# C rows of a Mamba scan: broadcast by DMA from DRAM in pairs, two states per GpSimd multiply

## What is computed

```python
def step(s, inp):
    d_t, u_t, B_t, C_t = inp
    dA = jnp.exp(d_t[..., None] * A)
    s = s * dA + (d_t * u_t)[..., None] * B_t[:, :, None, :]
    y_t = jnp.einsum('bhdn,bhn->bhd', s, C_t)
    return (s, y_t)
```

## Time and profile before

| | us |
|---|---|
| median of 3 runs | 6185.75 (6184.68 to 6187.2) |
| profiled execution, span | 6181.4 |
| VectorE busy | 6057.9 (98%) |
| GpSimd busy | 4848.8 (78%) |
| TensorE matmul busy | 4735.1 (77%) |
| ScalarE busy | 4198.7 (68%) |

### The profile page before, as it was taken

How to read it: one execution, slowest core, us unless ns; L and a number is a source line. 1 busy time by engine, 2 the same in 40 slices (tenths; PEclk the granted TensorE clock), 3 DMA queues, 4 the chain that set the end, 5 groups by cost and what they waited for, 6 DMA issues and landing times.

```text
span 6181.4 us, 90775 instructions
## 1 busy us (share of the span) xinstructions
PE 4735.1 (77%) x14623; PEld 2333.3 (38%) x14892; DVE 6057.9 (98%) x8285; ACT 4198.7 (68%) x7312; POOL 4848.8 (78%) x4113
## 2 busy tenths in 40 slices
PE   4777777777777777777777777777777777777778
PEld 1233333333333333333333333333333333333334
DVE  7999999999999999999999999999999999999998
ACT  5766766676666667666676676666766766676663
POOL 6888777777787778777777787777777877787875
PEclk9999999999999999999999999999999999999999
DMA  1000000000000000000000000000000000000000
GB/s 43 5 8 9 9 9 11 9 9 9 12 8 9 9 12 9 9 9 11 9 9 9 12 9 9 9 11 9 9 9 11 9 9 9 12 9 9 9 6 13
DMA packets 59893, 62.59 MB, mean 10 GB/s; under 512 B 7014, under 2 KB 58342, under 8 KB 59110
## 3 DMA queue, kind: packets, MB, share of 16 engines
q1 hardware_dynamic: 57536, 53.68, 2.8%
q10 hardware_dynamic: 1702, 2.16, 0.1%
HBM read 39.04 MB, written 16.78 MB: 9 GB/s over the span
## 4 chain that ended last, share of the span: by engine, by line
DVE 45%; issue 26%; PE 21%; DVEq 4%; ACT 3%; POOL 1%; another core or an unknown queue 0%; DMA 0%; ACTq 0%; POOLq 0%
DVE state L824 14%; DVE db L814 8%; DVE acc L763 8%; PE ybank L892 6%; PE pbank L901 3%; DVEq L97 3%; PE db L879 3%; PE bank_b L947 2%; DVE v L647 2%; DVE spw L708 2%; PE bank_a L1017 2%; ACT decay L408 1%; DVE hh L758 1%; PE cbank L870 1%; PE bank_a L980 1%
## 5 line engine op out<-in xcount | busy, mean ns | idle before, releaser
L558 POOL TENSOR_TENSOR prod<-state,cs 128x512 f32<-128x512 f32 x2048 | 2777.2, 1356 | 1068.2 <-DVE state L824 1025.6
L395 ACT ACTIVATE cs<-cbank 128x512 f32<-128x512 f32 x2048 | 1217.0, 594 | 1184.3 <-PE cbank L870 993.4
L408 ACT ACTIVATE decay<-delta,aneg 128x512 f32<-128x512 f32 x2048 | 1455.1, 716 | 607.2 <-DVE state L824 599.4
L879 PE MATMUL db<-pieces,sel 128*128 128x512 bf16 x2031 | 807.5, 398 | 1345.7 <-DVE state L824 1309.8
L892 PE MATMUL ybank<-prod,ident 128*128 128x512 f32 x3072 | 1626.7, 619 | 2.7 <-POOL prod L562 2.6
L814 DVE TENSOR_TENSOR db<-db,du 128x512 f32<-128x512 f32 x2048 | 1394.4, 681 | 46.8 <-PE db L879 28.3
L824 DVE TENSOR_TENSOR_SCAN state<-decay,carry,db 128x512 f32<-128x512 f32 x1024 | 1286.7, 1257 | 0.0
L824 DVE TENSOR_TENSOR_SCAN state<-decay,db 128x512 f32<-128x512 f32 x1024 | 1229.3, 1200 | 0.0
L879 PEld LDWEIGHTS db<-pieces,sel 128*128 128x128 bf16 x2048 | 199.5, 97 | 2245.9 <-DVE state L824 2157.8
L562 POOL TENSOR_TENSOR prod<-prod 128x512 f32<-128x512 f32 x512 | 690.7, 1349 | 40.1
L870 PE MATMUL cbank<-pieces,sel 128*128 128x512 bf16 x1797 | 699.2, 389 | 14.9 <-ACT cs L395 13.9
(11 more groups left out here) (125 smaller groups left out, 7017.3 us busy)
## 6 DMA issues: line engine op xcount, KB each, us to landing
xin<-in_hidden SPq DMA_DIRECT2D x128, 128.0 KB, 2.0
xres<-in_hidden SPq DMA_DIRECT2D x128, 128.0 KB, 2.1
out_x<-ot SPq DMA_DIRECT2D x128, 128.0 KB, 1.9
win<-in_win_t SPq DMA_DIRECT2D x1, 1024.0 KB, 10.3
sel<-in_sel SPq DMA_DIRECT2D x1, 1024.0 KB, 14.9
state<-in_w_gate ACTq DMA_DIRECT2D x1, 704.0 KB
state<-in_w_up ACTq DMA_DIRECT2D x1, 704.0 KB
yg<-in_w_down ACTq DMA_DIRECT2D x1, 704.0 KB, 18.3
```

Of the source, the lines that this page charges most:

```text
L395: act.activation(cs[:, gc.k % RING, :], cbank[:, :], ACT.Copy).then_inc(c_copied, 1)
L408: act.activation(decay[:, g.k % RING, :], delta[:, gu % 2, :], ACT.Exp, scale=aneg[:, gu % HEADS, gn:gn + 1]).then_inc(decayed, 1)
L558: pool.tensor_tensor(prod[:, gn % RING, :], state[:, gn, :], cs[:, gn % RING, :], ALU.mult).then_inc(weighted, 1)
L879: pe.matmul(db[DB_BANK[g.k % TRIP]][:, :], sel[:, gn, :], pieces[:, gu % 2, :], start=True, stop=True).then_inc(b_spread, 1)
```

## The change

The C rows of a unit leave SBUF by one small DMA into a DRAM buffer (`c_rows`), straight from the fp32 `xdbl`, and come back as eight DMAs of two rows each, broadcast over the 128 partitions, into `cs`, a ring of four pairs. SyncE issues them, at every odd step, each waiting until GpSimd has multiplied the pair that had the place before. TensorE's `cbank` matmuls, their ScalarE copies and the bank are gone. GpSimd multiplies two states by two C rows in one instruction of 1024 columns at every even step, into a ring of two pairs, and adds the two halves of pairs 0, 2, 4, 6. TensorE sums an added pair with one sum and another pair with two, 12 a unit as before. SyncE's three tile DMAs move from the unit's start to steps 2 and 15. VectorE's sum with D * u moves from step 2 to step 3 and writes `yg`, which GpSimd multiplies in place.

```diff
-PAIRED = (1, 6, 12, 14)
-YSUM_BACK = [(), (3, 2), (), ()] + [(3,)] * (NST - 4)
+PAIRS = NST // 2
+C_RING = 4
+P_RING = 2
+ADDED = (0, 2, 4, 6)
@@ SyncE
+            def spread_c(b, u, p):
+                slot = p % C_RING
+                free = held(sp, free_reg, u.val(PAIRS, p + 1 - C_RING))
+                if p == 0:
+                    rows_in = held(sp, rows_reg, u.val(16, 16))
+                    wait(sp, c_written, rows_in)
+                wait(sp, weighted, free)
+                rows = c_rows[u.mod(2), 2 * p:2 * p + 2, :].rearrange("n c -> (n c)")
+                sp.dma_start(cs[:, slot, :, :].rearrange("p n c -> p (n c)"),
+                             rows.unsqueeze(0).broadcast_to([P, 2 * CH])).then_inc(c_landed[slot], 16)
+            def step(b, j, n):
+                u, due = timetable(b, j, n)
+                if v := due("pre", 18):
+                    wait(sp, xd_evac, v.val(2, 2))
+                    sp.dma_start(c_rows[v.mod(2), :, :], xdbl[64:64 + NST, :]).then_inc(c_written, 16)
+                if n % 2:
+                    p = (n + 5) // 2
+                    w = u + p // PAIRS
+                    if w.within(UNITS):
+                        spread_c(b, w, p % PAIRS)
...
@@ ScalarE, step
-                gc = Ix(b, j * NST + n + 1, TRIP)
-                if gc.within(STEPS):
-                    wait(act, weighted, gc.val(plus=1 - RING))
-                    wait(act, c_spread, gc.val(plus=1))
-                    act.activation(cs[:, gc.k % RING, :], cbank[:, :], ACT.Copy).then_inc(c_copied, 1)
@@ GpSimd
+            def weigh(w, p):
+                c, r = p % C_RING, p % P_RING
+                wait(pool, scanned, w.val(NST, 2 * p + 2))
+                wait(pool, c_landed[c], w.val(16 * PAIRS // C_RING, 16 * (p // C_RING + 1)))
+                wait(pool, summed, w.val(PAIRS, p + 1 - P_RING))
+                pool.tensor_tensor(prod[:, r, :, :], state[:, 2 * p:2 * p + 2, :], cs[:, c, :, :],
+                                   ALU.mult).then_inc(weighted, 1)
+                if p in ADDED:
+                    wait(pool, weighted, w.val(PAIRS, p + 1))
+                    pool.tensor_tensor(prod[:, r, 0, :], prod[:, r, 0, :], prod[:, r, 1, :],
+                                       ALU.add).then_inc(added, 1)
             def step(b, j, n):
-                g = Ix(b, j * NST + n - 1, TRIP)
-                if g.within(STEPS):
...
+                if n % 2 == 0:
+                    w = u if n else u + -1
+                    if w.within(UNITS):
+                        weigh(w, (n - 2) // 2 % PAIRS)
@@ VectorE, between
-                if w := due("scan", 18):
-                    wait(dve, summed, w.val(NST, NST))
-                    wait(dve, yg_done, w.val())
-                    dve.scalar_tensor_tensor(yt[:, :], uu[:, w.mod(4), :], dsk[:, w.mod(HEADS):w.mod(HEADS) + 1],
+                if w := due("scan", 19):
+                    wait(dve, summed, w.val(PAIRS, PAIRS))
+                    wait(dve, op_mm, w.div(4, 4, -3))
+                    dve.scalar_tensor_tensor(yg[:, w.mod(8) // 4, w.mod(4), :], uu[:, w.mod(4), :], dsk[:, w.mod(HEADS):w.mod(HEADS) + 1],
                                              ybank[:, :], ALU.mult, ALU.add).then_inc(y_taken, 1)
@@ TensorE, step
-                for back in YSUM_BACK[n]:
-                    gy = Ix(b, j * NST + n - back, TRIP)
-                    if gy.within(STEPS) and gy.k % NST + 1 not in PAIRED:
-                        sum_up(b, gy)
+                if n % 2 == 0:
+                    w = u + (n - 4) // NST
+                    if w.within(UNITS):
+                        sum_up(w, (n - 4) // 2 % PAIRS)
                 side(b, u, due)
-                if g.within(STEPS):
-                    wait(pe, c_copied, g.val())
-                    pe.matmul(cbank[:, :], sel[:, NST + gn, :], pieces[:, gu % 2, :],
-                              start=True, stop=True).then_inc(c_spread, 1)
```

More of the change, by code:

```diff
@@ L102, in fresh, with held @@
     return b if isinstance(b, int) else eng.snap(b, min_val=1, max_val=BATCH - 2)
+def held(eng, reg, value):
+    if isinstance(value, int):
+        return value
+    eng.reg_mov(reg, value)
+    return reg
 def build(nc, hidden, win_t, conv_w, conv_b, xw, dtw, dt_b, a_log, dskip, wo_t, w_gate, w_up, w_down,
@@ L121, in build @@
         ident = sb("ident", [P])
-        sel = sb("sel", [2 * NST, P], BF16)
+        sel = sb("sel", [NST, P], BF16)
         less = sb("less", [2, P], BF16)
@@ L142, in build @@
         decay = sb("decay", [RING, CH])
-        cs = sb("cs", [RING, CH])
-        prod = sb("prod", [RING, CH])
+        cs = sb("cs", [C_RING, 2, CH])
+        prod = sb("prod", [P_RING, 2, CH])
         delta = sb("delta", [2, CH])
@@ L211, in build @@
         b_spread = sem("b_spread")
-        c_spread = sem("c_spread")
+        c_written = sem("c_written")
+        c_landed = [sem(f"c_landed{i}") for i in range(C_RING)]
         decayed = sem("decayed")
-        c_copied = sem("c_copied")
         db_done = sem("db_done")
@@ L285, in build @@
         w_tmp = [stage[2][0:WROWS, 0:GU_COLS], stage[3][0:WROWS, 0:GU_COLS], early[:, D_COLS:2 * D_COLS]]
-        w_scale = [prod[0:rows, w, 0:3 * P].rearrange("p (a b) -> p a b", a=3)[:, :, 0:cols // BLK]
+        w_scale = [prod[0:rows, :, :].rearrange("p r t c -> p (r t) c")[:, w, 0:3 * P].rearrange("p (a b) -> p a b", a=3)[:, :, 0:cols // BLK]
                    for w, (rows, cols) in enumerate(((WROWS, GU_COLS), (WROWS, GU_COLS), (P, D_COLS)))]
@@ L351, in unit @@
             def unit(b, j):
                 b = fresh(sp, b)
[L353 to L364, removed]
+                for n in range(NST):
+                    step(b, j, n)
             trips(sp, unit, constants)
@@ L475, in step @@
                     wait(act, res_mm, v.val(2))
+                    wait(act, c_written, v.val(16))
                     act.activation(hi[:, :], pbank[:, :], ACT.Copy).then_inc(xd_evac, 1)
@@ L880, in spread_b, with sum_up @@
                           start=True, stop=True).then_inc(b_spread, 1)
-            def sum_up(b, g):
-                gu, gn = Ix(b, g.k // NST, PER), g.k % NST
-                first = gn == 0 or gn == 1 and 1 in PAIRED
-                if first:
-                    wait(pe, y_taken, gu.val())
-                if gn in PAIRED:
-                    wait(pe, paired, gu.val(len(PAIRED), PAIRED.index(gn) + 1))
-                else:
-                    wait(pe, weighted, g.val(plus=1))
-                pe.matmul(ybank[:, :], ident[:, :], prod[:, gn % RING, :],
-                          start=first, stop=(gn == NST - 1)).then_inc(summed, 2 if gn in PAIRED else 1)
+            def sum_up(w, p):
+                if p == 0:
+                    wait(pe, y_taken, w.val())
+                if p in ADDED:
+                    wait(pe, added, w.val(len(ADDED), ADDED.index(p) + 1))
+                else:
+                    wait(pe, weighted, w.val(PAIRS, p + 1))
+                for k in range(1 if p in ADDED else 2):
+                    last = pe.matmul(ybank[:, :], ident[:, :], prod[:, p % P_RING, k, :],
+                                     start=(p == 0), stop=(p == PAIRS - 1 and k == 1))
+                last.then_inc(summed, 1)
             def side(b, u, due):
```

47 lines of the change are left out of this document (25 added, 22 removed).

## The result

| | before | changed |
|---|---|---|
| median us | 6185.3 (6184.68 to 6187.2) | 6631.87 (6626.49 to 6636.56) |
| ratio to before | | 1.0722, 95% interval 1.0706 to 1.0737 |
| profiled span us | 6181.4 | 6634.4 |
| mean granted TensorE clock | 0.96 | 0.88 |

A forecast was written before the change was run, and what follows sets the result against it. VectorE was taken as the bound, busy for 98% of the span. 6181.4 + 295 for longer holds + 5 for the remaining units + 24 for TensorE behind scan 1 gave 6505 us, median 6510, range 6240 to 6700.

The forecast's parts named there:

- The bound and the rule: VectorE bounds; its two-SBUF-operand and one-operand fp32 operations wait for a whole GpSimd operation under way, 6.4 us a unit.
- the walk: One unit in program order, VectorE's unheld distances plus holds: 8.86 us held for 6.39, so 50.06 us instead of 47.59.
- The multiply: GpSimd's multiply of two states, 1024 columns: 2.35 us, at most 2.54, instead of two of 1.27.
- `hw<-hh`: VectorE, 5.64 us after scan 13 starts: waits for L600, then held by the next multiply; loses 3.00 us for 0.85.
- `vw<-v`: VectorE, 6.0 us after scan 5 starts: GpSimd's multiply goes first by 0.3 us; loses 1.92 us for 0.
- `hw<-hw`, `v` L647: VectorE operations that meet an idle GpSimd: 0 us held instead of 1.06 and 0.85.
- The taps: VectorE's convolution taps behind scan 9: first held 2.10 us for 1.04, second 0.43 for 1.01, third 0.43 for 0.
- TensorE behind scan 1: Step 2: pair 7's two sums, 2.0 us, precede the gate matmul; 0.2 us a unit within 0 to 0.5, 24 us.
- the sentence that the next `db` was spread before: TensorE behind scan 1: the lost cover would cost no more than the 24 us already taken.
- DMA: 1024 broadcasts of 512 KB: some 28% of 16 engines' span, at slowest 5.2 us each; cost taken as 0.
- TensorE and ScalarE relieved: 2048 matmuls and 2048 copies taken away: worth between 0 and 28 us, taken as 0.
- Rival (a): Both order races, at `hw<-hh` and `vw<-v`, go the other way: 46.5 us a unit, 6054 us, faster; chance 7%.

The follow-up runs named there:

- the moved kernel: The changed kernel with VectorE's roundings of `hw`, `hh` and `v` moved to where GpSimd stands still, and L600 ahead of step 14's pair: 6065.52 us, ratio 0.981.
- The pairs alone: The changed kernel with C by TensorE and ScalarE as before, no C DMA, `cs` a ring of two pairs: 6713.28 us, ratio 1.0852.

## Why the prediction was right, point by point

- **The bound and the rule.** Held operations were the 6.4 us to watch. The order that the walk gave came out at every place but the first tap, and the sum of the holds came out as a whole: by the distances between starts, as a mean of 108 units of the loop, VectorE lost 2.43 us a unit more to GpSimd than before (L600's wait counted in), where the walk has 8.86 - 6.39 = 2.47. That it is so near is in part luck, as the taps' error is covered by others.
- **The multiply.** Expected 2.35 to 2.6 us; it is 2.35 unheld, 2393 ns as a mean.
- **`hw<-hh`.** From scan 13 to scan 0 the walk gives 9.08 us with 3.00 lost; the unit shown has 3192.94 - 3183.77 = 9.17.
- **`vw<-v`.** 1.92 us lost by the walk, 2.05 in the mean (2.25 us between starts for 0.20).
- **`hw<-hw`, `v` L647.** Free, as said: 1.9 us a unit of recovered holds, 1.06 and 0.83 as means.
- **The taps.** Here the walk missed in half of the units. It had the first tap behind the multiply; in the unit shown it went ahead, only the second was held, and scan 9 to scan 10 took 4.93 us instead of 5.9. That gave back 1.0 us there, and `spl`, now later, held `spw` for 0.44 us that the walk had at 0. As a mean of the loop's units, in half of which the multiply won as the walk says, the first two taps lost 2.0 us where it had 2.5, and `spw` 0.2 to 0.3 where it had 0.
- **TensorE behind scan 1 is the term that was mis-sized.** I took 0.2 us a unit in 0 to 0.5, 24 us in sum. VectorE's waits for TensorE's `db` and `ybank` are 184.7 us in the changed kernel and 43.9 before (the 28.3 of the earlier trace rows and the two lines below), so 141 us more, and that is nearly the whole difference of 122 us between 6510 and 6632: with 141 for 24 the sum is 6622 for the span, and 6634.4 was measured.

```profile
DVE db L814 <- issue: 9.8, 5, 2.1
DVE yt L682 <- PE ybank L892: 5.8, 4, 1.5
```

  Of the changed kernel's waits 94 us are behind scans 2 and 3: 27 for `ybank` and 67 for `db`, 0.8 us a unit. The step that failed is the sentence that the next `db` was spread before: the one for scan 4 was, but the one for scan 5 stands on TensorE behind both sums, the transposes and the gate matmuls. I had followed the chain to ScalarE's tanh and not the queue behind the sums. I also took the clock's loss from the stretch of before, which was 0.64 behind pauses of 0.9 and 2.4 us, and not from longer pauses: my own walk had `hw<-hh` 2.15 us later, and the diff leaves TensorE one matmul in step 1. It became 0.54. With the pauses filled these 94 us are gone, and 88 us of the time.

  The other 48 us are `db` behind scan 15, 82 us for 34, a place to which the walk gave no wait at all. Half of them are at the loop's seam, in one unit of each batch row, where the changed kernel has two sums ahead of that `db` (first the kernel before, then the changed one):

```profile
3071.48 0.70 DVE L814 TENSOR_TENSOR db<-db,du 128x512 f32<-128x512 f32 x1 [1.80 <-PE db L879]
...
3289.96 3.21 PE L926 MATMUL ybank<-prod,ident 128*128 128x512 f32 x4
3295.38 0.70 DVE L853 TENSOR_TENSOR db<-db,du 128x512 f32<-128x512 f32 x1 [3.29 <-PE db L914]
```

  The matmuls in the pauses of steps 0 and 1 did not take this wait away; it fell only with one sum there instead of two (pair 5 added, in the moved kernel).
- **DMA.** 26.6% of the engines' span where 28% was estimated, a landing in 3.6 us where up to 5.2 was allowed, and GpSimd's multiply never among the waits for it. The bytes' 0 to 45 us were not in the sum.
- **TensorE and ScalarE relieved: taken as 0.** The pairs alone say 81 us, since the pairs make the other engines' slack scarce behind scan 1. With the waits of before alone this could not be read off.

The unit came to 51.1 us (median in the loop) where the walk gave 50.06 and 49.5. Rival (a), faster, needed VectorE to come to both places outside of a multiply. By moving the operations that was made so, and it is faster.

## What to carry to other kernels

Where VectorE and GpSimd both work on SBUF, look at the spread of one instruction form's duration before counting busy time: 6.4 of 47.6 us a unit were waiting inside of instructions. A longer GpSimd instruction saves its own start-up and lengthens every hold, but it also leaves longer free stretches; it pays only if the sharing VectorE operations are moved into them, so write down for each where the other engine is when it is dispatched. When an engine becomes less loaded, ask what its pauses do to its clock, and go down its queue past the instruction that you moved to the one that the bound engine waits for.

## What the runs showed of the hardware

- Of two instructions that share, the one dispatched first runs and the other is held: 3190.37 behind 3190.30 held `hw<-hh`, and 2792.76 behind 2792.70 the copy of `carry`. Where the recorded starts are 0.01 to 0.02 us apart it goes either way: the multiply was held at 3221.18 and the tap at 3425.83, both with the tap recorded first.
- A VectorE operation that waits on the semaphore of a GpSimd instruction loses to the GpSimd instruction directly behind it (3190.37, 2.65 us for 0.53).
- A broadcast of the same 4 KB to 128 partitions costs no more than loading different rows: 594 MB in 26.6% of 16 engines' span, where the 54 MB of before took 2.8%, and 512 KB landed in 3.6 us.
- A 1024-column multiply of two SBUF tiles on GpSimd takes 2.35 us where a 512-column one takes 1.27: pairing saves 0.19 us.
- Behind pauses of 2.65 and some 3.3 us with one matmul between them the granted clock was 0.50 for 6.0 us of busy TensorE. Matmuls in the pause, not beside it, restore it (0.88 to 0.94, and 0.91 to 0.99 in the moved kernel), and a fixed number in every step did not (0.89). The Trainium skill, "TensorE: Matmul & The Clock Gate", section "Part 1: The HAM clock gate", has the two clock levels and a return to the higher one only behind sustained work. The trace agrees: 0.50 up to 3203.9 and 1.00 from there, with TensorE busy since 3197.93.
